# Gathering: VectorE subtracts the maxima of four of a unit's 32 experts in place, TensorE's second shift product is 384 columns wide

## The chip, the cores and the metric

The kernel runs on one core of a Trainium2 chip. The core has TensorE (matrix products; the profile calls its products PE and its weight loads PEld), VectorE (DVE), ScalarE (ACT), GpSimd (POOL) and SyncE (SP), which here only starts transfers. Each engine works through its own list of instructions in order, and semaphores are the only thing that holds one engine for another. The metric is the device time of one execution in microseconds (us), from the first to the last instruction of the core, and a little around it; less is better.

## The reference, cut to what matters

The program is one decoder block over 64 x 128 = 8192 tokens of 128 features: self attention, cross attention, and a layer of soft slots ("soft mixture of experts") with 64 experts of 32 slots each. The change lies in the last layer, in the softmax D over the slots of an expert, which weighs the tokens that are gathered into the slots:

```
logits = (jnp.einsum('tzd,ed->tze', x, phi_w) + phi_b).reshape(t, z, n, p)   # n = 64 experts, p = 32 slots
D = jax.nn.softmax(logits, axis=3)
C = jax.nn.softmax(logits, axis=2)
X_tilde = jnp.einsum('tznp,tzd->npd', D, x)
...
Y = jnp.einsum('tznp,npH->tzH', C, Y_tilde)
```

A softmax subtracts the largest logit of its group before the exponential. In D the group is the 32 slots of one expert, for each token.

## The kernel before, in words

The stages follow one another: attention, cross attention, `gather_slots` (logits, D and X_tilde), `run_experts`, `mix_slots` (C, Y and the last norm). The change touches `gather_slots` alone.

`gather_slots` goes through 128 units: 64 tiles of 128 tokens, two units to a tile, each with 32 of the 64 experts (1024 of the 2048 logits of a token). The logits of a unit lie in `psL[u % 2]`, two banks of PSUM of 512 columns: bank 0 holds the unit's experts 0 to 15, bank 1 its experts 16 to 31, 32 columns to an expert. The names in the trace are `gather_` and the name in the code (`gather_L` is `psL`, `gather_e` is `e`), and `slots_X` is `psX`, where X_tilde is summed over all tiles.

A unit u passes through these steps:

- TensorE L1009: six products of 512 columns make the logits (three terms for each bank, since x and the weights are each split into a high and a low part). The last one counts `l_made`.
- ScalarE L1035 copies half of each bank's raw logits to `keep`, bank 1 first and bank 0 after VectorE's first maximum; SyncE L993 stores them for the stage `mix_slots`. Each copy counts `kept`.
- VectorE L1067 and L1069 take the maximum of each expert's 32 slots, bank 0 and bank 1, into `mx` (count `mx_ready`).
- TensorE L1016 subtracts the maxima: two products, one a bank, of the negated identity `w.neg_ident` with `mx` spread out 32 times over (16 x 32 = 512 columns), added onto the logits in PSUM. They wait for `mx_ready` and `kept` and count `shifted`.
- ScalarE L1046 takes the exponential of both banks into `e` (count `e_ready`), VectorE L1073 sums it, waits for its own sum and inverts it (L1077, `rinv`), and GpSimd L1098 multiplies into `d`.
- The first half of `d` is split into a high part (ScalarE L1058, `dh`) and a low part (GpSimd L1092, `dl`), and so is x: ScalarE L1055 makes `x2h` and VectorE L1083 `x2l`, once a tile.
- TensorE adds to X_tilde: L1023 in full float32 with the second half of `d` (one product in the code, two instructions in the trace), L1028 to L1030 with the split parts.

The order is written by hand. In step k of the loop TensorE does the logits of unit k, the shift of unit k-1 and the sums L1023 to L1030 of unit k-4. VectorE does the maxima of unit k, then the sum and inverse of unit k-1, then `x2l` of unit k-2 where k is even. ScalarE does `keep` bank 1 of unit k, the exponential of k-1, `keep` bank 0 of k, `x2h` and `dh` of k-2. GpSimd does `dl` of unit k-3, then `d` of unit k-1. Of the waits between the steps three matter here: L1009 of unit k waits for the exponential of unit k-2 (`psL` has two halves), L1028 waits for `dl` and `x2l`, and L1073 for the exponential.

`Mix.peaks` (L1324 to L1338, in the stage `mix_slots`) is not touched. It is of interest since VectorE there subtracts maxima in place for a whole bank (L1337), right after two maxima (L1328, L1332).

Of the kernel before, what the change touches and what calls it, by code (L numbers as in the profile page):

```python
# [18 lines left out]
ALU = mybir.AluOpType  # L19
ACT = mybir.ActivationFunctionType  # L20
X = mybir.AxisListType.X
F32 = mybir.dt.float32
# [33 lines left out]
def reach(eng, sem, value):  # L56

    if not isinstance(value, int) or value > 0:
        eng.wait_ge(sem, value)  # L59
# [887 lines left out]
def gather_slots(nc, io, w, psX):  # L947
# [4 lines left out]
    TILES = TOKENS // 128  # L952
    UNITS = 2 * TILES
    KEEPS = 3
    WE_EVERY, WE_PART = UNITS // 16, EXPERTS // 16
    with ExitStack() as ctx:
        st = Store(nc, ctx, "gather")
        mx = [st.sb(f"mx{i}", [128, 2, 16], F32R) for i in range(2)]
# [8 lines left out]
        dl = [st.sb(f"dl{i}", [128, 512], F32R) for i in range(2)]  # L967
        keep = [st.sb(f"keep{i}", [128, SLOTS - MADE, 32]) for i in range(KEEPS)]
        psL = [st.ps(f"L{i}", [128, 2, 512]) for i in range(2)]
# [4 lines left out]
         x_made) = (  # L974
            st.sem(n) for n in ("l_made", "low_max", "mx_ready", "kept", "shifted", "e_ready", "sum_done", "rinv_ready",
                                "d_ready", "d_read", "dh_ready", "dl_ready", "x_made"))
        stored = [st.sem(f"stored{i}") for i in range(KEEPS)]
        block = ctx.enter_context(nc.Block())

        def units(k, lag):  # L980
            return [k - lag] if 0 <= k - lag < UNITS else []

        def rows(u):
            return slice(u // 2 * 128, u // 2 * 128 + 128)
# [3 lines left out]
        @block.sync  # L988
        def _(sync):
            by_row = io["expert_w"].rearrange("n d h -> d n h")  # L990
            for u in range(UNITS):
                sync.wait_ge(kept, 2 * u + 2)
                sync.dma_start(w.kept[rows(u), u % 2], keep[u % KEEPS][:]).then_inc(stored[u % KEEPS], 16)  # L993
                if u % WE_EVERY == WE_EVERY - 1:
                    some = slice(u // WE_EVERY * WE_PART, (u // WE_EVERY + 1) * WE_PART)
                    sync.dma_start(w.we[:, some, :], by_row[:, some, :]).then_inc(w.we_loaded, 16)
            sync.dma_start(w.beT[:], io["expert_bT"]).then_inc(w.be_loaded, 16)
            for i in range(KEEPS):
                sync.wait_ge(stored[i], 16 * len(range(i, UNITS, KEEPS)))

        @block.tensor
        def _(pe):
            for k in ORDER:
                for u in units(k, 0):
                    reach(pe, e_ready, u - 1)
                    for n, (xs, ws) in enumerate(((w.xh, w.w1h), (w.xl, w.w1h), (w.xh, w.w1l))):
                        for i in range(2):
                            c = (2 * (u % 2) + i) * 512
                            ins = pe.matmul(psL[u % 2][:, i, :], xs[:, rows(u)], ws[:, c:c + 512],  # L1009
                                            start=n == 0, stop=n == 2)  # L1010
                    ins.then_inc(l_made, 1)
                for u in units(k, 1):
                    pe.wait_ge(mx_ready, u + 1)
                    pe.wait_ge(kept, 2 * u + 2)
                    for i in range(2):
                        ins = pe.matmul(psL[u % 2][:, i, :], w.neg_ident[:],  # L1016
                                        mx[u % 2][:, i, :].unsqueeze(2).to_broadcast([128, 16, 32]), start=False,
                                        stop=True, skip_group_check=True)
                    ins.then_inc(shifted, 1)
                for u in units(k, 4):  # L1020
                    t, j, first, last = u // 2, u % 2, u < 2, u >= UNITS - 2
                    pe.wait_ge(d_ready, u + 1)
                    pe.matmul(psX[:, 2 * j + 1, :], w.xres[:, rows(u)], dd[u % 4][:, 1, :], start=first, stop=last)\  # L1023
                        .then_inc(d_read, 1)
                    pe.wait_ge(x2l_ready, t + 1)
                    pe.wait_ge(dl_ready, u + 1)
                    out = psX[:, 2 * j, :]
                    pe.matmul(out, x2h[t % 2][:], dh[j][:], start=first, stop=False)  # L1028
                    pe.matmul(out, x2h[t % 2][:], dl[j][:], start=False, stop=False)
                    pe.matmul(out, x2l[t % 2][:], dh[j][:], start=False, stop=last).then_inc(x_made, 1)  # L1030

        @block.scalar
        def _(act):
            def keep_bank(u, i):
                act.copy(keep[u % KEEPS][:, :, 16 * i:16 * i + 16],  # L1035
                         psL[u % 2][:, i, :].rearrange("t (n p) -> t p n", n=16)[:, MADE:SLOTS, :]).then_inc(kept, 1)
# [23 lines left out]
        @block.vector  # L1060
        def _(dve):
            for k in ORDER:
                for u in units(k, 0):
                    by_expert = psL[u % 2][:].rearrange("p i (n s) -> p i n s", n=16)
                    dve.wait_ge(l_made, u + 1)
                    reach(dve, shifted, u - 1)
                    dve.tensor_reduce(mx[u % 2][:, 0, :], by_expert[:, 0], X, ALU.max).then_inc(low_max, 1)  # L1067
                    dve.wait_ge(kept, 2 * u + 1)
                    dve.tensor_reduce(mx[u % 2][:, 1, :], by_expert[:, 1], X, ALU.max).then_inc(mx_ready, 1)  # L1069
                for u in units(k, 1):  # L1070
                    dve.wait_ge(e_ready, u + 1)
                    reach(dve, rinv_ready, u - 1)
                    dve.tensor_reduce(rsum[u % 2][:].rearrange("p (i n) -> p i n", i=2), e[u % 2][:], X, ALU.add)\  # L1073
                        .then_inc(sum_done, 1)
                    dve.wait_ge(sum_done, u + 1)
                    reach(dve, d_ready, u - 1)
                    dve.reciprocal(rinv[u % 2][:], rsum[u % 2][:]).then_inc(rinv_ready, 1)  # L1077
                for u in units(k, 2):
                    t = u // 2
                    if u % 2 == 0:  # L1080
                        dve.wait_ge(x2h_ready, t + 1)
                        reach(dve, x_made, u - 2)
                        dve.tensor_tensor(x2l[t % 2][:], w.xres[:, rows(u)], x2h[t % 2][:], ALU.subtract)\  # L1083
                            .then_inc(x2l_ready, 1)
# [416 lines left out]
def decoder_block(nc, io, out):  # L1501
    with ExitStack() as ctx:
# [58 lines left out]
        with ExitStack() as banks:  # L1561
            sl = Store(nc, banks, "slots")
            psX = sl.ps("X", [128, 4, 512])
            w.we = sl.sb("we", [128, EXPERTS, 128])
            w.beT = sl.sb("beT", [128, EXPERTS])
            gather_slots(nc, io, w, psX)
            w1_space.close()
            with ExitStack() as spaces:
                mix = Mix(nc, spaces, w, psX)
                run_experts(nc, w, psX, mix)  # L1570
                mix_slots(nc, w, mix, out)
# [32 lines left out]
```

## Time and profile before

| | |
|---|---|
| median of 3 runs | 1380.32 us (1377.62 to 1383.22) |
| the profiled execution | 1381.27 us |
| its span, first to last instruction | 1379.2 us |
| gathering, first to last logits product of TensorE | 458.0 to 887 us |
| TensorE products busy, whole span | 1286.2 us (93%) |
| VectorE, ScalarE, GpSimd busy | 1105.5, 896.5, 1162.0 us (80%, 65%, 84%) |
| TensorE's granted clock, mean | 0.983 of full speed |

The rows come from one profiled execution. Times are microseconds from the start of the span. In a timeline each row is one instruction, or several of the same kind merged (x2), with its start, its length and, in brackets, the idle time of its engine before it and what ended that. A product of TensorE starts while the one ahead of it still drains, so a product's length (0.39) is more than its share of the engine; the share is read from start to start. On VectorE and GpSimd too an instruction that waits for nothing starts up to 0.09 us before the end recorded for the one ahead of it.

### The profile page before, as it was taken

How to read it: one execution, taken by the hardware profiler on the slowest of the kernel's cores; microseconds unless marked ns; L12 is line 12 of the kernel's file. 1: busy time of each engine (PE TensorE's matmuls, PEld its weight loads, DVE VectorE, ACT ScalarE, POOL GpSimd, SP SyncE). 2: the span in 40 equal slices, each digit the busy share in tenths (PEclk: the TensorE clock that was granted, in tenths of full speed). 3: DMA queues.
4: the chain of work that ended last, by engine and by line, in shares of the span. 5: the costliest groups of instructions: out<-in, count | busy, mean ns of one | idle time of the engine just before them, and what ended most of it. 6: DMA issues, size and time to landing. Idle time of an engine off the chain costs nothing. (4 is left out here: it accounts for less than half of the span.)

```text
span 1379.2 us, 31693 instructions
## 1 busy us (share of the span) xinstructions
PE 1286.2 (93%) x11006; PEld 1050.8 (76%) x11006; DVE 1105.5 (80%) x2462; ACT 896.5 (65%) x1670; POOL 1162.0 (84%) x1044
## 2 busy tenths in 40 slices
PE   6785899999998799999999999969999999999998
PEld 5664677777776577777777777659999999999997
DVE  4997466666666788888888888878999999999996
ACT  3996566666666477767777677645666666666664
POOL 3666587888886599999999999958999999999997
PEclk9997899999999999999999999999999999999999
DMA  4222434434341122222222222212222222232321
GB/s 111 79 83 76 131 112 121 123 111 132 112 122 52 54 92 84 85 89 95 85 84 92 92 85 85 85 60 83 88 86 83 91 79 95 74 100 70 103 70 32
DMA packets 90963, 123.74 MB, mean 90 GB/s; under 512 B 8803, under 2 KB 62628, under 8 KB 90804
## 3 DMA queue, kind: packets, MB, share of 16 engines
q1 hardware_dynamic: 90294, 121.49, 27.9%
q8 instruction: 90, 1.47, 0.5%
q14 instruction: 67, 0.55, 0.1%
q10 hardware_dynamic: 512, 0.23, 0.1%
HBM read 70.41 MB, written 51.33 MB: 88 GB/s over the span
## 5 line engine op out<-in xcount | busy, mean ns | idle before, releaser
L1098 POOL TENSOR_TENSOR gather_d<-gather_e,gather_rinv 128x1024 f32<-128x1024 f32 x128 | 245.2, 1915 | 35.9 <-DVE gather_rinv L1077 35.9
L1357 POOL TENSOR_TENSOR mix_c<-mix_e,mix_rinv 128x1024 f32<-128x1024 f32 x128 | 241.1, 1904 | 17.9 <-DVE mix_rinv L1345 16.0
L1425 PEld LDWEIGHTS last_Y<-kept_phi,last_cT 128*128 128x128 f32 x2048 | 248.3, 192 | 7.2
L1425 PE MATMUL last_Y<-kept_phi,last_cT 128*128 128x128 f32 x2048 | 249.1, 275 | 0.0
L1441 ACT COPY last_cT<-last_T 128x1024 f32<-128x1024 f32 x128 | 128.5, 1004 | 132.4 <-PE last_T L1432 132.4
L920 POOL TENSOR_TENSOR cross_kd<-first_pack,kept_consts 128x624 fp32r<-128x624 f32 x128 | 155.7, 1238 | 59.7 <-DMA first_pack<-first_halves 54.3
L819 DVE TENSOR_REDUCE cross_mx<-cross_S 128x8 fp32r<-128x624 f32 x128 | 103.6, 809 | 107.9 <-PE cross_S L637 107.9
L1342 DVE TENSOR_REDUCE mix_sums<-mix_e 128x16 f32<-128x1024 f32 x128 | 155.8, 1217 | 34.4 <-ACT mix_e L1316 34.0
L1073 DVE TENSOR_REDUCE gather_rsum<-gather_e 128x32 f32<-128x1024 f32 x128 | 156.1, 1220 | 25.8 <-ACT gather_e L1046 25.8
L1092 POOL TENSOR_TENSOR gather_dl<-gather_d,gather_dh 128x512 fp32r<-128x512 f32 x128 | 166.3, 1299 | 0.0
L1035 ACT COPY gather_keep<-gather_L 128x256 f32<-128x256 f32 x256 | 94.8, 370 | 95.7 <-PE gather_L L1009 95.3
L1432 PE MATMUL last_T<-kept_consts,mix_c 128*128 128x128 f32 x1024 | 134.6, 275 | 3.2 <-POOL mix_c L1357 1.1
L1046 ACT ACTIVATE gather_e<-gather_L 128x1024 f32<-128x1024 f32 x128 | 131.1, 1025 | 7.4
L741 ACT ACTIVATE cross_pT<-cross_P 77x1024 f32<-77x1024 f32 x128 | 131.3, 1029 | 0.6 <-PE cross_P L657 0.6
L1023 PE MATMUL slots_X<-gather_d,kept_xres 128*128 128x512 f32 x256 | 130.7, 592 | 0.0
L1350 POOL TENSOR_TENSOR mix_less<-mix_read,mix_high 128x1024 f32<-128x1024 f32 x64 | 122.6, 1916 | 7.4 <-DVE mix_high L1332 4.1
L1432 PEld LDWEIGHTS last_T<-kept_consts,mix_c 128*128 128x128 f32 x1024 | 114.8, 142 | 4.5 <-issue 2.5
L1067 DVE TENSOR_REDUCE gather_mx<-gather_L 128x16 fp32r<-128x512 f32 x128 | 88.6, 692 | 29.6 <-PE gather_L L1009 20.7
L1028 PE MATMUL slots_X<-gather_dh,gather_x2h 128*128 128x512 f32 x128 | 101.0, 789 | 2.9 <-DVE gather_x2l L1083 1.5
L1058 ACT CAST gather_dh<-gather_d 128x512 fp32r<-128x512 f32 x128 | 79.5, 621 | 31.4 <-PE slots_X L1030 19.6
L1069 DVE TENSOR_REDUCE gather_mx<-gather_L 128x16 fp32r<-128x512 f32 x128 | 87.2, 681 | 0.0
L1009 PE MATMUL gather_L<-over_w1h,kept_xh 128*128 128x512 f32 x256 | 81.5, 400 | 4.3 <-ACT gather_e L1046 3.3
(205 smaller groups left out, 2979.6 us busy)
## 6 DMA issues: line engine op xcount, KB each, us to landing
kept_logits<-gather_keep SPq DMA_DIRECT2D x128, 256.0 KB, 2.0
mix_read<-kept_logits SPq DMA_DIRECT2D x64, 512.0 KB, 3.8
first_halves<-first_qk SPq DMA_DIRECT2D x32, 412.0 KB, 3.2
first_pack<-first_halves SPq DMA_DIRECT2D x64, 128.0 KB
first_pack<-first_halves SPq DMA_DIRECT2D x32, 206.0 KB
first_pack<-first_halves SPq DMA_DIRECT2D x64, 78.0 KB
first_xTg<-in_xT SPq DMA_DIRECT2D x16, 256.0 KB, 2.8
kept_xres<-in_x SPq DMA_DIRECT2D x16, 256.0 KB, 3.2
```

What stands on the lines that cost most here:

```text
L741: act.activation(pT[n % 2][0:J, hs, :, :], psP[:, hs, :, :], ACT.Exp)\
L920: pool.tensor_tensor(kd[n % 2][:, q], keys[:, q].to_broadcast([128, 2, 4, JP]), w.own.unsqueeze(1).unsqueeze(3).to_broadcast([128, 2, 4, J ...
L1023: pe.matmul(psX[:, 2 * j + 1, :], w.xres[:, rows(u)], dd[u % 4][:, 1, :], start=first, stop=last)\
L1046: act.activation(e[u % 2][:], psL[u % 2][:].rearrange("p i (n s) -> p i n s", n=16), ACT.Exp)\
L1073: dve.tensor_reduce(rsum[u % 2][:].rearrange("p (i n) -> p i n", i=2), e[u % 2][:], X, ALU.add)\
L1092: pool.tensor_tensor(dl[u % 2][:], dd[u % 4][:, 0, :], dh[u % 2][:], ALU.subtract).then_inc(dl_ready, 1)
L1098: pool.tensor_tensor(dd[u % 4][:].rearrange("p i (n s) -> p i n s", n=16), e[u % 2][:], rinv[u % 2][:].rearrange("p (i n) -> p i n", i=2). ...
L1342: dve.tensor_reduce(self.sums[u % 2][:], self.e[u % 2][:], X, ALU.add).then_inc(self.sum_done, 1)
L1357: pool.tensor_tensor(self.cc[u % 2][:], self.e[u % 2][:], self.rinv[u % 2][:].unsqueeze(2).to_broadcast([128, 16, EXPERTS]), ALU.mult)\
L1425: ins = pe.matmul(psY[t % 2][:, 0:128], cT[u % 2][:, c, :], w.yk[:, 8 * (u % 2) + c, :], start=(u % 2 == 0 and c == 0), stop=(u % 2 == 1 a ...
L1432: ins = pe.transpose(psT[:, c, :], mix.cc[u % 2][:, 2 * c:2 * c + 2, :], w.ident)
L1441: act.copy(cT[u % 2][:], psT[:]).then_inc(cT_ready, 1)
```

## The change

After the maxima of a unit VectorE waits for its own second maximum and then subtracts, in place in PSUM, the maxima of the unit's last four experts (experts 12 to 15 of bank 1, 4 x 32 = 128 columns). TensorE's second shift product covers the other twelve experts of that bank, 384 columns instead of 512. The first one keeps 512. TensorE waits for VectorE's new count `lowered` in place of `mx_ready`. Nothing else is different. The lines after the change are 2 higher up to the shift products and 6 higher behind VectorE's new instruction.

```diff
+    SHIFTED = 16 - 4
...
+        lowered = st.sem("lowered")
...
                 for u in units(k, 1):
-                    pe.wait_ge(mx_ready, u + 1)
+                    pe.wait_ge(lowered, u + 1)
                     pe.wait_ge(kept, 2 * u + 2)
-                    for i in range(2):
-                        ins = pe.matmul(psL[u % 2][:, i, :], w.neg_ident[:],
-                                        mx[u % 2][:, i, :].unsqueeze(2).to_broadcast([128, 16, 32]), start=False,
+                    for i, n in enumerate((16, SHIFTED)):
+                        ins = pe.matmul(psL[u % 2][:, i, 0:32 * n], w.neg_ident[:],
+                                        mx[u % 2][:, i, 0:n].unsqueeze(2).to_broadcast([128, n, 32]), start=False,
                                         stop=True, skip_group_check=True)
                     ins.then_inc(shifted, 1)
...
                     dve.tensor_reduce(mx[u % 2][:, 1, :], by_expert[:, 1], X, ALU.max).then_inc(mx_ready, 1)
+                    dve.wait_ge(mx_ready, u + 1)
+                    rest = by_expert[:, 1, SHIFTED:16]
+                    dve.tensor_tensor(rest, rest, mx[u % 2][:, 1, SHIFTED:16].bitcast(F32).unsqueeze(2)
+                                      .to_broadcast([128, 16 - SHIFTED, 32]), ALU.subtract).then_inc(lowered, 1)
```

VectorE's list in the middle of the gathering, before, from the inverse of one unit to the inverse of the second one after it:

```order
L1077 RECIPROCAL gather_rinv<-gather_rsum 128x32 [waits gather_d_ready,gather_sum_done]
L1067 TENSOR_REDUCE gather_mx<-gather_L 128x16 [waits gather_shifted,gather_l_made]
L1069 TENSOR_REDUCE gather_mx<-gather_L 128x16 [waits gather_kept]
L1073 TENSOR_REDUCE gather_rsum<-gather_e 128x32 [waits gather_rinv_ready,gather_e_ready]
L1077 RECIPROCAL gather_rinv<-gather_rsum 128x32 [waits gather_d_ready,gather_sum_done]
L1083 TENSOR_TENSOR gather_x2l<-kept_xres,gather_x2h 128x128 [waits gather_x_made,gather_x2h_ready]
```

The same place now:

```order
L1083 RECIPROCAL gather_rinv<-gather_rsum 128x32 [waits gather_d_ready,gather_sum_done]
L1069 TENSOR_REDUCE gather_mx<-gather_L 128x16 [waits gather_shifted,gather_l_made]
L1071 TENSOR_REDUCE gather_mx<-gather_L 128x16 [waits gather_kept]
L1074 TENSOR_TENSOR gather_L<-gather_L,gather_mx 128x128 [waits gather_mx_ready]
L1079 TENSOR_REDUCE gather_rsum<-gather_e 128x32 [waits gather_rinv_ready,gather_e_ready]
L1083 RECIPROCAL gather_rinv<-gather_rsum 128x32 [waits gather_d_ready,gather_sum_done]
L1089 TENSOR_TENSOR gather_x2l<-kept_xres,gather_x2h 128x128 [waits gather_x_made,gather_x2h_ready]
```

The new instruction stands between the maxima of unit k and the sum of unit k-1, and all that VectorE does later in the step stands behind it.

TensorE's list for one step of the loop, before:

```order
L1009 MATMUL gather_L<-over_w1l,kept_xh 128x512 x2
L1016 MATMUL gather_L<-gather_mx,kept_neg_ident 128x512 [waits gather_kept,gather_mx_ready]
L1016 MATMUL gather_L<-gather_mx,kept_neg_ident 128x512
L1023 MATMUL slots_X<-gather_d,kept_xres 128x512 [waits gather_d_ready]
L1028 MATMUL slots_X<-gather_dh,gather_x2h 128x512 [waits gather_dl_ready,gather_x2l_ready]
L1029 MATMUL slots_X<-gather_dl,gather_x2h 128x512
L1030 MATMUL slots_X<-gather_dh,gather_x2l 128x512
L1009 MATMUL gather_L<-over_w1h,kept_xh 128x512 [waits gather_e_ready]
```

And now:

```order
L1011 MATMUL gather_L<-over_w1l,kept_xh 128x512 x2
L1018 MATMUL gather_L<-gather_mx,kept_neg_ident 128x512 [waits gather_kept,gather_lowered]
L1018 MATMUL gather_L<-gather_mx,kept_neg_ident 128x384
L1025 MATMUL slots_X<-gather_d,kept_xres 128x512 [waits gather_d_ready]
L1030 MATMUL slots_X<-gather_dh,gather_x2h 128x512 [waits gather_dl_ready,gather_x2l_ready]
L1031 MATMUL slots_X<-gather_dl,gather_x2h 128x512
L1032 MATMUL slots_X<-gather_dh,gather_x2l 128x512
L1011 MATMUL gather_L<-over_w1h,kept_xh 128x512 [waits gather_e_ready]
```

Nothing moved on TensorE: one product has 384 columns for 512, and one wait has another name. ScalarE, GpSimd and SyncE have the same instructions in the same order as before.

## Rows read from the trace of the kernel before

**Rows 1.** Busy time by stretch: engines in order, TensorE's clock, DMA.

```profile
core 0: us, PE busy (x) PEld busy (x) DVE busy (x) ACT busy (x) POOL busy (x), PEclk, DMA share, GB/s
...
700.00:800.00 100.00, 100.00 (x388) 72.67 (x387) 86.81 (x134) 70.19 (x135) 93.87 (x61) 1.00 0.25 90
```

**Rows 2.** Who waited for whom, 471 to 889 us: total, times, longest.

```profile
POOL gather_d L1098 <- DVE gather_rinv L1077: 26.2, 123, 1.3
DVE gather_rsum L1073 <- ACT gather_e L1046: 24.7, 124, 0.2
```

**Rows 3.** Timeline of TensorE's products, one step of the loop.

```profile
703.79 0.63 PE L1009 MATMUL gather_L<-over_w1h,kept_xh 128*128 128x512 f32 x2
...
704.72 0.63 PE L1009 MATMUL gather_L<-over_w1l,kept_xh 128*128 128x512 f32 x2
705.18 0.59 PE L1016 MATMUL gather_L<-gather_mx,kept_neg_ident 128*128 128x512 f32 x2
705.62 1.02 PE L1023 MATMUL slots_X<-gather_d,kept_xres 128*128 128x512 f32 x2
...
706.93 0.40 PE L1030 MATMUL slots_X<-gather_dh,gather_x2l 128*128 128x512 f32 x1
707.17 0.62 PE L1009 MATMUL gather_L<-over_w1h,kept_xh 128*128 128x512 f32 x2
```

**Rows 4.** Timeline of cross attention: products of 312 columns, one narrower behind.

```profile
301.18 0.52 PE L637 MATMUL cross_S<-cross_kd,first_pack 128*128 128x312 f32 x2
301.54 0.38 PE L619 MATMUL cross_P<-first_xo,cross_oT 128*128 128x128 f32 x2
...
301.40 0.33 PEld L619 LDWEIGHTS cross_P<-first_xo,cross_oT 128*128 128x128 f32 x2
```

**Rows 5.** Timeline of the other engines, the same step of the loop.

```profile
702.00 0.69 DVE L1067 TENSOR_REDUCE gather_mx<-gather_L 128x16 fp32r<-128x512 f32 x1 [0.28 <-PE gather_L L1009]
...
702.43 1.02 ACT L1046 ACTIVATE gather_e<-gather_L 128x1024 f32<-128x1024 f32 x1
702.61 0.68 DVE L1069 TENSOR_REDUCE gather_mx<-gather_L 128x16 fp32r<-128x512 f32 x1
...
703.49 1.22 DVE L1073 TENSOR_REDUCE gather_rsum<-gather_e 128x32 f32<-128x1024 f32 x1 [0.20 <-ACT gather_e L1046]
703.56 0.42 PEld L1009 LDWEIGHTS gather_L<-over_w1h,kept_xh 128*128 128x128 f32 x2
...
703.68 1.31 POOL L1092 TENSOR_TENSOR gather_dl<-gather_d,gather_dh 128x512 fp32r<-128x512 f32 x1
...
704.75 0.35 DVE L1077 RECIPROCAL gather_rinv<-gather_rsum 128x32 f32<-128x32 f32 x1
...
705.01 0.23 DVE L1083 TENSOR_TENSOR gather_x2l<-kept_xres,gather_x2h 128x128 fp32r<-128x128 f32 x1
705.18 1.92 POOL L1098 TENSOR_TENSOR gather_d<-gather_e,gather_rinv 128x1024 f32<-128x1024 f32 x1 [0.20 <-DVE gather_rinv L1077]
```

**Rows 6.** VectorE's subtractions out of PSUM, by line and form, whole span.

```profile
L1337 DVE TENSOR_TENSOR slots_X<-slots_X,mix_mx 128x512 f32<-128x512 f32 x64 | 44.1, 690 | 0.0
L826 DVE TENSOR_TENSOR cross_y<-cross_P,kept_xres 128x128 f32<-128x128 f32 x61 | 17.1, 281 | 0.0
```

**Rows 7.** The start of the gathering: timeline, engines mixed.

```profile
461.58 0.68 DVE L1069 TENSOR_REDUCE gather_mx<-gather_L 128x16 fp32r<-128x512 f32 x1
...
462.57 0.59 PE L1016 MATMUL gather_L<-gather_mx,kept_neg_ident 128*128 128x512 f32 x2
...
464.28 0.73 PE L1009 MATMUL gather_L<-over_w1h,kept_xh 128*128 128x512 f32 x2 [1.11 <-ACT gather_e L1046]
...
467.49 0.73 PE L1009 MATMUL gather_L<-over_w1h,kept_xh 128*128 128x512 f32 x2 [1.11 <-ACT gather_e L1046]
```

**Rows 8.** Timeline, the last `x2l`, beside GpSimd's `dl`.

```profile
892.77 1.26 POOL L1092 TENSOR_TENSOR gather_dl<-gather_d,gather_dh 128x512 fp32r<-128x512 f32 x1
...
892.88 1.30 DVE L1083 TENSOR_TENSOR gather_x2l<-kept_xres,gather_x2h 128x128 fp32r<-128x128 f32 x1
893.99 1.96 POOL L1098 TENSOR_TENSOR gather_d<-gather_e,gather_rinv 128x1024 f32<-128x1024 f32 x1
```

## The prediction

> **What bounds the kernel now.** The change touches one stage, so I first read the table of busy time by stretch for that stage. In the 100 us from 700 to 800 TensorE is busy for all 100.00 us at its full granted clock (1.00, the 2.4 GHz level), GpSimd for 93.87, VectorE for 86.81, ScalarE for 70.19 [rows 1]. A busy TensorE may still be one that is held back in small pieces, so the second view is the timeline of its products. One step of the loop lasts from 703.79 to 707.17, 3.38 us [rows 3]. In it the six logits products take 1.39 us (703.79 to 705.18), 0.23 each, and the two shift products 0.44 us (705.18 to 705.62), 0.22 each. At 2.4 GHz 512 columns need 0.213 us, so nothing waits inside these groups; the rest of the step, 1.55 us (705.62 to 707.17), holds the full float32 product, which runs its columns four times (0.85), and three more of 0.23 (0.69), 1.54 in sum. So the step is TensorE's columns, and no wait is left in it. Third, the table of waits for 471 to 889 us: GpSimd waits 26.2 us for the inverse L1077, 0.21 us in each of 123 units, and VectorE 24.7 us for the exponential [rows 2]. Those are engines with room that wait for a step set elsewhere. A column taken from TensorE should therefore shorten the step, as long as the others keep their room.
>
> **TensorE's part.** Each unit loses 128 columns of one product. At 2.4 GHz that is 128 / 2.4 = 53 ns. The trace has no product of 384 columns in this place. The nearest rows from above are the shift products of 512 themselves, 0.22 us each [rows 3]. From below it is a product of 312 columns in cross attention: its successor's weight load begins at 301.40, as it itself begins, and the successor's product at 301.54, so 312 columns with their overhead took 0.14 us [rows 4]. From there 72 columns more are 0.03, which puts the product of 384 at 0.17 us and the gain at 0.045 to 0.05. From the 512 it is 0.16 to 0.167 and the gain 0.053. I take 0.053, since that row is the same instruction with the same operands, and keep 0.045 for the range. Over 128 units: 6.8 us, or 5.8 at the lower bound.
>
> The Trainium skill has a rule that speaks against this: "TensorE: Matmul & The Clock Gate", section "Back-to-back issue gap", gives sustained spacings of about 131 ns for 512 columns and 81 ns for 128, which is 17 ns for each 128 columns; by that the sum would be an estimated 2.1 us. The shift products' 0.22 us for 512 columns does not agree with its 131 [rows 3]; the same section's other formula, N/2.4 + 2.5 ns, does, and gives 6.8.
>
> **VectorE's part.** One instruction is added in each unit: 128 columns, one input in PSUM and one in SBUF, written to PSUM. A subtraction of this shape out of PSUM into SBUF takes 0.281 us, and the in-place one of 512 columns 0.690 [rows 6]; the slope between them is 1.07 ns a column, so the two forms lie on one line and the in-place write should cost little. I take 0.28; bounds are 0.23 (the `x2l` subtraction out of SBUF [rows 5]) and 0.35. It waits for VectorE's own last result. The sum and the inverse stand in the same relation: 703.49 + 1.22 = 704.71, and the inverse begins at 704.75 [rows 5], so 0.04 is added. Behind it the sum starts up to 0.08 before its recorded end, as L1069 does behind L1067 (702.00 + 0.69 against 702.61). Net: 0.28 + 0.04 - 0.08, about 0.24 us a unit on VectorE.
>
> Where does it fall? Counted from the start of L1067 (702.00), the second maximum ends at 1.29, the subtraction runs from 1.33 to 1.61, and the sum could start at 1.53. Before it started at 1.49, held by the exponential (702.43 + 1.02 = 703.45) [rows 5]. The exponential now ends 0.053 earlier after L1067, at 1.40. So what ends last before the sum is the new subtraction, and the sum is late by some 0.04 us against before. Then 1.22 + 0.04 + 0.35 for sum and inverse: the inverse ends at 3.14, and in a unit with `x2l` that ends at 3.14 - 0.09 + 0.23 = 3.28, with the next maximum possible from 3.20. In the other units it is possible from 3.05. The new step is 3.38 - 0.053 = 3.325. VectorE keeps 0.12 us in even units and 0.27 in odd ones; it stays hidden. If the subtraction took 0.35, even units would keep 0.05.
>
> **Who waits behind it.** TensorE: the shift of unit k-1 is issued a step later than its maxima. The maxima of the unit begin at 702.00, `lowered` would come at about 703.6, and its shift products start at 705.18 [rows 3, 5]: 1.5 us of room, so the new wait costs nothing. GpSimd: L1098 waits for the inverse (0.20 us idle before it at 705.18) and moves 0.04 later with it; from its start to the end of L1092 behind it is 1.92 + 1.31 less an overlap of about 0.04, 3.19 us against a step of 3.325 [rows 5]. It keeps some 0.13 us. TensorE's L1009 waits for the exponential, which ends at 703.45, while the weight load for L1009 comes at 703.56 [rows 5]; both move with the shift products, so those 0.1 us stay. ScalarE and SyncE get nothing new.
>
> **Ends of the stage.** The first steps are not bound by columns: L1009 starts at 464.28 and 467.49, a step of 3.21 us, after waits of 1.11 us for the exponential [rows 7]. In that loop the shift products lie too, so 0.053 is saved there as well. In the very first unit the second maximum ends at 461.58 + 0.68 = 462.26 and the shift starts at 462.57 [rows 7]; with 0.04 + 0.28 for the subtraction and a little for the signal it moves to about 462.65: 0.1 us lost once. At the end the last inverses are late by 0.04 once. Together 0.15 us. The later stages have the same work and start earlier.
>
> **The sum.** 6.8 - 0.15 = 6.6 us. Against the profiled execution: span 1379.2 - 6.6 = 1372.6, with the 2.1 us around it 1374.7. The profiled execution (1381.27) is 0.95 us above the median, so against the median I forecast 1380.32 - 6.6 = 1373.7 us. A measurement of this kernel can tell about 0.5% from no change, here 6.9 us, or 1373.4: my forecast is 0.48% and lies right at that line.
>
> **Rivals.**
>
> 1. *The weight load becomes the floor.* A weight load of 128 columns is recorded with 0.19 us (0.42 for two that start 0.23 apart [rows 5]), longer than the 0.16 of the new product. If the product behind could not start before its load's recorded end, the slot would be 0.19 and the gain 0.03 a unit, 3.8 us: 1376.5. Against it: at 301.40 such a load begins and the product that uses it starts 0.14 us later [rows 4].
>
> 2. *Another engine takes over the step.* GpSimd and VectorE have only some 0.13 us left. Should the subtraction and its waits cost VectorE 0.4 us a unit and not 0.24, the even units alone would grow and eat the gain of the odd ones: about 1380, no change. For it: VectorE's room is the smallest of all. Against it: each term has a row of its own kind.
>
> 3. *Slower: `x2l` meets GpSimd.* `x2l` (L1083) reads two operands from SBUF. At 892.88 it was issued while GpSimd's L1092 ran (892.77 to 894.03) and took 1.30 us, not 0.23: it sat until that one was nearly over [rows 8]. In the steady state it falls into the gap that GpSimd leaves while it waits for the inverse: L1092 ends at 704.99, `x2l` runs from 705.01, L1098 starts at 705.18 [rows 5]. This gap shrinks by 0.05. If L1098 came to read first, `x2l` would wait for all of it, and 1.9 - 0.12 = 1.8 us would be added to every second unit: 64 x 1.8 = 115 us, 1489. It decides at `x2l` being issued after L1098, which means 0.17 us later against it than now. Both follow the same inverse, so their distance stays, and at 892.88 the waiting `x2l` ended at 894.18, well inside L1098 (893.99 to 895.95), so it was served first [rows 8]. I expect it to be met by the end of L1092 at worst, for hundredths.
>
> The Trainium skill states the mechanism ("SBUF — State Buffer", section "Who interferes with whom"): a VectorE instruction with two SBUF inputs contends with GpSimd instructions that read SBUF, and who starts first holds the other off. The row at 892.88 agrees. By the same section the new subtraction, with one input in PSUM, is not concerned.
>
> **How the numbers follow.** Forecast mechanism (TensorE's columns, 5.7 to 7.0 us): 0.80. Rival 1: 0.08. Rival 2: 0.07. Rival 3: 0.05. The three runs before lie from 2.7 below to 2.9 above their median, and a median of new runs may be off by some 1.5. The forecast's 6.6 against the line at 6.9 puts the 0.80 at about one half each: 0.40 faster by over 0.5%, 0.40 within. Rivals 1 and 2 are within 0.5% (0.15), though 0.01 of rival 2 is slower. So faster 0.40, same 0.54, slower 0.06. Range: from 1373.7 - 0.4 - 2.7 = 1370.6 to rival 1 with some scatter, 1376.5 + 2.1 = 1378.6; rivals 2 and 3 are left out.
>
> **What would show it.** The step of TensorE in the middle of the stage is 3.32 to 3.33 us, and the second shift product's slot 0.16; the weight load's floor would show as 0.19 with a step of 3.35. The new VectorE instruction reads 0.27 to 0.30 us. The idle time before the sum moves from the exponential to nothing, and `x2l` stays near 0.23. GpSimd's wait for the inverse falls from 0.21 to about 0.15. If `x2l` reads well over 0.3 us, rival 3 is at work; if TensorE waits for `lowered`, my room of 1.5 us was wrong. The logits products would end some 6.6 us earlier, and every later stage be unchanged in length.

## The result: 1372.96 us, and the profile after

| | before | after |
|---|---|---|
| median of 6 runs | 1380.1 us (1377.62 to 1383.22) | 1372.96 us (1368.54 to 1375.12) |
| ratio, 95% interval | | 0.995 (0.9938 to 0.9963) |
| span of the profiled execution | 1379.2 us | 1371.7 us |
| first and last start of the first maximum (L1067, now L1069) | 461.0 and 887.7 us | 460.2 and 880.4 us |

The forecast was 1373.7 us, 6.6 less than before; the medians differ by 7.1. The last row of the table holds the gathering, from its first unit to its last: 426.7 us before and 420.2 now, 6.5 less. Between these two profiled executions another 0.8 us lies before the stage began, where both kernels have the same code, and 0.2 behind it.

Where the 6.5 us went is seen in the timeline of TensorE's products in the changed kernel, one step of the loop (L1011 makes the logits, L1018 is the shift, L1025 the float32 product, L1030 to L1032 the split ones):

```profile
704.07 0.54 PE L1018 MATMUL gather_L<-gather_mx,kept_neg_ident 128*128 128x512 f32 x2
704.44 1.02 PE L1025 MATMUL slots_X<-gather_d,kept_xres 128*128 128x512 f32 x2
704.90 0.80 PE L1030 MATMUL slots_X<-gather_dh,gather_x2h 128*128 128x512 f32 x1
705.54 0.40 PE L1031 MATMUL slots_X<-gather_dl,gather_x2h 128*128 128x512 f32 x1
705.77 0.40 PE L1032 MATMUL slots_X<-gather_dh,gather_x2l 128*128 128x512 f32 x1
706.01 0.62 PE L1011 MATMUL gather_L<-over_w1h,kept_xh 128*128 128x512 f32 x2
706.46 0.63 PE L1011 MATMUL gather_L<-over_w1h,kept_xl 128*128 128x512 f32 x2
706.93 0.62 PE L1011 MATMUL gather_L<-over_w1l,kept_xh 128*128 128x512 f32 x2
707.39 0.54 PE L1018 MATMUL gather_L<-gather_mx,kept_neg_ident 128*128 128x512 f32 x2
```

The step is 707.39 - 704.07 = 3.32 us, where [rows 3] had 3.38. The two shift products take 704.07 to 704.44, 0.37 us and not 0.44; the merged row names only the first one's 512 columns. Everything else has its old spacing. TensorE is busy for the whole stretch as before:

```profile
core 0: us, PE busy (x) PEld busy (x) DVE busy (x) ACT busy (x) POOL busy (x), PEclk, DMA share, GB/s
700.00:800.00 100.00, 100.00 (x393) 72.94 (x393) 94.25 (x166) 71.65 (x136) 95.38 (x61) 1.00 0.24 88
```

Against [rows 1] VectorE rose from 86.81 to 94.25 us of 100, and GpSimd from 93.87 to 95.38, since its same work now fits into shorter steps. VectorE and GpSimd in the same step:

```profile
703.72 0.35 DVE L1083 RECIPROCAL gather_rinv<-gather_rsum 128x32 f32<-128x32 f32 x1
...
704.15 1.91 POOL L1104 TENSOR_TENSOR gather_d<-gather_e,gather_rinv 128x1024 f32<-128x1024 f32 x1 [0.16 <-DVE gather_rinv L1083]
...
704.26 0.69 DVE L1069 TENSOR_REDUCE gather_mx<-gather_L 128x16 fp32r<-128x512 f32 x1 [0.19 <-PE gather_L L1011]
...
704.87 0.68 DVE L1071 TENSOR_REDUCE gather_mx<-gather_L 128x16 fp32r<-128x512 f32 x1
...
705.59 0.30 DVE L1074 TENSOR_TENSOR gather_L<-gather_L,gather_mx 128x128 f32<-128x128 f32 x1
...
705.80 1.21 DVE L1079 TENSOR_REDUCE gather_rsum<-gather_e 128x32 f32<-128x1024 f32 x1
...
707.04 0.35 DVE L1083 RECIPROCAL gather_rinv<-gather_rsum 128x32 f32<-128x32 f32 x1
...
707.31 0.23 DVE L1089 TENSOR_TENSOR gather_x2l<-kept_xres,gather_x2h 128x128 fp32r<-128x128 f32 x1
```

The new subtraction takes 0.30 us, starts 0.04 behind the end of the maximum ahead of it (704.87 + 0.68 = 705.55), and the sum follows without a wait. In [rows 5] the sum started 1.49 us after the first maximum; now it is 705.80 - 704.26 = 1.54. The table of waits, 471 to 882 us, says who still waits; against [rows 2] the sum's wait for the exponential is gone, and GpSimd's wait for the inverse is listed for 86 units where it was for 123:

```profile
POOL gather_d L1104 <- DVE gather_rinv L1083: 13.4, 86, 0.2
DVE gather_mx L1069 <- PE gather_L L1011: 11.7, 61, 0.2
```

The view leaves out waits under 0.15 us. Over the units 8 to 119 GpSimd sat idle before `d` for 0.204 us in the mean before the change and for 0.154 after it.

### The profile page after: what moved, and what is told of

It reads as the page before. It is cut to its first block and busy times, and to the rows that moved or that the text cites. A ratio compares the mean times of both kernels' runs of the same rounds, so it can differ in the third digit from the quotient of the medians.

```text
span 1371.7 us, 31821 instructions
## 1 busy us (share of the span) xinstructions
PE 1279.5 (93%) x11006; PEld 1048.0 (76%) x11006; DVE 1129.5 (82%) x2590; ACT 896.0 (65%) x1670; POOL 1160.2 (85%) x1044
## 5 line engine op out<-in xcount | busy, mean ns | idle before, releaser
L1025 PE MATMUL slots_X<-gather_d,kept_xres 128*128 128x512 f32 x256 | 130.8, 593 | 0.0
L1069 DVE TENSOR_REDUCE gather_mx<-gather_L 128x16 fp32r<-128x512 f32 x128 | 88.5, 692 | 18.6 <-PE gather_L L1011 15.3
L1030 PE MATMUL slots_X<-gather_dh,gather_x2h 128*128 128x512 f32 x128 | 101.0, 789 | 2.9 <-POOL gather_dl L1098 2.9
L1011 PE MATMUL gather_L<-over_w1h,kept_xh 128*128 128x512 f32 x256 | 80.9, 398 | 4.3 <-ACT gather_e L1048 3.3
```

## The experiments

The main theory is that of the prediction: the step of the gathering is TensorE's columns, and VectorE's subtraction is hidden. The rivals were a cost of the subtraction on the path, the weight load as a floor, another engine taking over, and `x2l` meeting GpSimd. In the tables "step" is the mean distance from one start of the first maximum to the next over the units 5 to 123 of the profiled execution, 3.377 us before and 3.323 after the change. Ratios are against the kernel before on the same chip, whose median there was 1378.96 us for the first four runs (four experts with 512 columns, 384 columns alone, eight experts, the whole bank), 1380.4 for 256 and 64 columns alone, and 1379.77 for the others.

### Each half of the change alone

First, the subtraction on VectorE with the product of 512 columns kept:

```diff
-                    for i, n in enumerate((16, SHIFTED)):
+                    for i, n in enumerate((16, 16)):
```

> VectorE subtracts the four experts' maxima as in the changed kernel, and TensorE's second shift product keeps its 512 columns (so the four experts are shifted twice, which a softmax does not notice). Theory (the step of the gathering is TensorE's columns, VectorE's new instruction is hidden): the step stays at 3.38 us and the time at that of the kernel before, 1380 us, ratio 0.998 to 1.002. Rival (VectorE's instruction costs something on the path): over 1382 us, and TensorE or GpSimd waits longer.

Measured: 1379.71 us, ratio 1.0005 (0.9992 to 1.0017), step 3.377 us. Second, the narrow product with nobody subtracting the rest:

```diff
-                    pe.wait_ge(lowered, u + 1)
+                    pe.wait_ge(mx_ready, u + 1)
...
-                    dve.wait_ge(mx_ready, u + 1)
-                    rest = by_expert[:, 1, SHIFTED:16]
-                    dve.tensor_tensor(rest, rest, mx[u % 2][:, 1, SHIFTED:16].bitcast(F32).unsqueeze(2)
-                                      .to_broadcast([128, 16 - SHIFTED, 32]), ALU.subtract).then_inc(lowered, 1)
```

> TensorE's second shift product has 384 columns and nobody subtracts the maxima of the other four experts: that part of the shift is left out. Theory (columns alone): the step is 3.32 us and the time that of the changed kernel, 1373 us, within 1 us. Rival (VectorE's subtraction costs part of the gain): this one is faster than the changed kernel by 2 us or more.

Measured: 1371.23 us, ratio 0.9944 (0.9929 to 0.9958), step 3.323 us, the same to the nanosecond as that of the changed kernel. The two ratios, 0.9944 here and 0.995 for the change, lie within each other's intervals. The median is 1.7 us lower than that of the changed kernel and the "within 1 us" of the expectation was missed. The kernel before is 1.1 us lower in this comparison too (1378.96 against 1380.1), the runs scatter by some 3 us, and the stage is not shorter (L1069's first and last start):

```profile
L1069 DVE TENSOR_REDUCE gather_mx<-gather_L x128: 690/692/692, 459.3 to 880.0; 128x16 fp32r<-128x512 f32 x128
```

That is 420.7 us, against 420.2 with the subtraction. The whole gain is in the columns, and the subtraction costs nothing that these runs can show. The waits of the first experiment (subtraction and 512 columns) show the same from the other side: GpSimd's wait for the inverse is back at 0.21 us a unit (25.0 us in 119), as in [rows 2].

```profile
POOL gather_d L1104 <- DVE gather_rinv L1083: 25.0, 119, 0.2
```

### More experts on VectorE: how far the room goes

The runs with eight and with six experts are the changed kernel with another number in one line, for eight:

```diff
-    SHIFTED = 16 - 4
+    SHIFTED = 16 - 8
```

> As the changed kernel, with eight experts on VectorE and 256 columns in the second product. Theory: TensorE's step is 3.323 - 0.053 = 3.27 us; VectorE needs 0.13 us more a unit, 3.33 in even and 3.18 in odd units, 3.26 in the mean, so it has just no room left and does not yet set the step; 1366.5 us, ratio 0.990. Rival (VectorE's even units count one by one, or GpSimd is pushed): a step of 3.30 us or more, 1370 us or above.

> As the changed kernel, with six experts on VectorE and 320 columns in the second product. Theory: TensorE's columns set the step at 3.323 - 0.027 = 3.297 us, VectorE needs 3.27 and 3.11 us in even and odd units; 1370 us, ratio 0.993. Rival (the even units with x2l already hold the step): 3.32 us and 1373 us.

| experts on VectorE, columns of the second product | time | ratio (95%) | step |
|---|---|---|---|
| 4, 384 (the change) | 1372.96 | 0.995 (0.9938 to 0.9963) | 3.323 |
| 6, 320 | 1369.48 | 0.9924 (0.9912 to 0.9937) | 3.295 |
| 8, 256 | 1368.83 | 0.9922 (0.9909 to 0.9934) | 3.278 |
| 16, none | 1394.36 | 1.0107 (1.0094 to 1.0121) | 3.476 |

With six the step is what the columns give (3.297 was expected). With eight it is 3.278 where 3.27 was expected. Its time missed the expected 1366.5 us by 2.3: the stage, from the first maximum to the last, takes 414.98 us against 420.24 in the changed kernel, 5.3 less and not 6.8, and the rest is within the scatter of the medians. By their times six and eight cannot be told apart. With eight the step is no longer even: the distances from maximum to maximum alternate between 3.164 and 3.392 us (means over odd and even units). VectorE is now the one without room, and it meets GpSimd. Timeline of VectorE and GpSimd in the run with eight:

```profile
701.54 1.92 POOL L1104 TENSOR_TENSOR gather_d<-gather_e,gather_rinv 128x1024 f32<-128x1024 f32 x1 [0.23 <-DVE gather_rinv L1083]
...
703.41 1.28 POOL L1098 TENSOR_TENSOR gather_dl<-gather_d,gather_dh 128x512 fp32r<-128x512 f32 x1
...
704.48 0.35 DVE L1089 TENSOR_TENSOR gather_x2l<-kept_xres,gather_x2h 128x128 fp32r<-128x128 f32 x1
704.65 1.97 POOL L1104 TENSOR_TENSOR gather_d<-gather_e,gather_rinv 128x1024 f32<-128x1024 f32 x1
704.76 0.68 DVE L1069 TENSOR_REDUCE gather_mx<-gather_L 128x16 fp32r<-128x512 f32 x1
```

`x2l` is issued at 704.48, while GpSimd's `dl` (703.41 to 704.69) still runs; it takes 0.35 us and not 0.23, and GpSimd's next product is recorded with 1.97 and not 1.92. VectorE loses 0.12 us and GpSimd 0.05 in every second unit, and the mean step is only 0.005 us over that of 256 columns with nothing on VectorE (3.273, below).

All sixteen experts of the bank on VectorE, without the second product:

```diff
-    SHIFTED = 16 - 4
+    SHIFTED = 16 - 16
...
-                    for i, n in enumerate((16, SHIFTED)):
+                    for i, n in enumerate((16,)):
```

> As the changed kernel, with all sixteen experts of bank 1 on VectorE and no second product. Theory: TensorE's columns would allow 3.38 - 0.22 = 3.16 us, but VectorE's subtraction grows from 0.30 to 0.69 us and VectorE needs 3.59 and 3.43 us in even and odd units; the step is 3.51 us and the time 1380 + 128 x 0.13 = 1397 us, ratio 1.012. Rival (columns alone count): 3.19 us, held by GpSimd, 1356 us.

Measured: 1394.36 us, ratio 1.0107, step 3.476 us. Here VectorE sets the step alone: its subtraction is 0.70 us, and TensorE waits for it in each unit. From the table of waits of that run, 471 to 880 us:

```profile
POOL gather_d L1104 <- DVE gather_rinv L1083: 39.5, 118, 1.5
ACT gather_keep L1037 <- DVE gather_mx L1069: 35.8, 118, 0.3
PEld gather_L L1018 <- DVE gather_L L1074: 26.9, 118, 0.3
```

The expected 3.51 was 0.035 too long. The first maximum is recorded with 0.653 us in the mean here against 0.692, which is about as much; both it and the second (0.68) follow at once on other work here. Steps of 3.431 and 3.520 alternate.

The last of this group asks whether a single unit in which VectorE is too slow holds the step, or only the mean. VectorE subtracts eight experts and TensorE keeps 384 columns:

```diff
-    SHIFTED = 16 - 4
+    SHIFTED = 16 - 8
...
-                    for i, n in enumerate((16, SHIFTED)):
+                    for i, n in enumerate((16, 12)):
```

> VectorE subtracts eight experts as in the run with eight, TensorE's second product keeps 384 columns (four of the eight are shifted twice, which a softmax does not notice). VectorE needs 3.33 us in even and 3.18 us in odd units against 3.323 of TensorE. If only the mean over two units counts, the step stays at 3.323 and the time at 1373 us. If an even unit that is too long holds TensorE, the step alternates and its mean is over 3.33 us, 1374 us or more.

Measured: 1374.82 us, ratio 0.9966 (0.9954 to 0.9979), step 3.321 us. VectorE needs an estimated 3.33 us in every second unit and the mean step is still TensorE's 3.32. A margin of 0.01 us is thin by itself. The run with eight experts and 256 columns says it more clearly: its long units take 3.392 us, 0.12 over TensorE's 3.273, and the mean of long and short is 3.278. So the mean over two units counts. In the run with 384 columns VectorE is busy for 97.05 of the 100 us from 700 to 800, 2.8 more than after the change, and the step is the same. The time is 1.8 us over the expectation of 1373, within the scatter of the runs; the stage takes 420.4 us against 420.2 in the changed kernel, so the profile shows no cause for it there.

### What `x2l` costs when it meets GpSimd

In the changed kernel `x2l` keeps its length (min/median/max in ns, 64 of them):

```profile
L1089 DVE TENSOR_TENSOR gather_x2l<-kept_xres,gather_x2h x64: 226/228/334, 468.4 to 885.5; 128x128 fp32r<-128x128 f32 x64
```

So the rival did not occur, and its price was made visible by moving `x2l` between the two maxima of the next step (the last tile's `x2l` is done apart):

```diff
                     dve.tensor_reduce(mx[u % 2][:, 0, :], by_expert[:, 0], X, ALU.max).then_inc(low_max, 1)
+                    if k % 2 == 1 and k >= 3:
+                        t = (k - 3) // 2
+                        dve.wait_ge(x2h_ready, t + 1)
+                        reach(dve, x_made, 2 * t - 2)
+                        dve.tensor_tensor(x2l[t % 2][:], w.xres[:, rows(2 * t)], x2h[t % 2][:], ALU.subtract)\
+                            .then_inc(x2l_ready, 1)
...
-                        dve.tensor_tensor(x2l[t % 2][:], w.xres[:, rows(u)], x2h[t % 2][:], ALU.subtract)\
-                            .then_inc(x2l_ready, 1)
```

> As the changed kernel, with VectorE's x2l issued in the next step, between its two maxima, when GpSimd is in the middle of its product d. This pays the price of the rival in which x2l meets GpSimd. If x2l waits for the whole of d: x2l is recorded with 1.1 to 1.6 us, VectorE needs 7.4 to 7.6 us for two units, the step is 3.7 to 3.85 us in the mean and the time 1420 to 1440 us. If two inputs in SBUF do not collide with GpSimd here, x2l stays at 0.23 us and the time at 1373 us.

Measured: 1440.04 us, ratio 1.0429 (1.0412 to 1.0445), step 3.850 us, 4.725 and 2.975 in turn. Timeline of GpSimd and VectorE:

```profile
699.62 1.92 POOL L1108 TENSOR_TENSOR gather_d<-gather_e,gather_rinv 128x1024 f32<-128x1024 f32 x1
699.86 1.82 DVE L1074 TENSOR_TENSOR gather_x2l<-kept_xres,gather_x2h 128x128 fp32r<-128x128 f32 x1
...
701.50 1.32 POOL L1102 TENSOR_TENSOR gather_dl<-gather_d,gather_dh 128x512 fp32r<-128x512 f32 x1
...
701.61 0.68 DVE L1077 TENSOR_REDUCE gather_mx<-gather_L 128x16 fp32r<-128x512 f32 x1
```

`x2l` was issued 0.24 us behind the start of GpSimd's `d` and ended at 701.68, 0.14 behind its end: 1.82 us for an instruction of 0.23, more than the 1.1 to 1.6 that were expected; the step and the time lie at the upper end of what was expected. The maxima (0.63 to 0.68) and the sums (1.21), with one input, run beside GpSimd no longer than usual. The same instruction issued 0.16 us ahead of `d`, as in the changed kernel, costs nothing that shows, and 0.24 behind it the whole kernel takes 67 us more than the changed one. It was said ahead of the prediction that semaphores are the only thing that holds one engine for another; [rows 8] and this run show an engine that is held without one.

### The floor under a short product

With the rest of the shift left out and VectorE out of the question, how short can the second product become?

```diff
-    SHIFTED = 16 - 4
+    SHIFTED = 16 - 12
```

(16 - 8 and 16 - 14 for the other two, each also without VectorE's subtraction, as in the second experiment.)

> TensorE's second product has 128 columns and nobody subtracts the maxima of the other twelve experts, which leaves that part of the shift out. It looks for the next bound behind the columns. TensorE's columns alone would give 3.38 - 0.16 = 3.217 us and 1359.6 us. GpSimd needs 1.915 + 1.30 - 0.04 - 0.04 = 3.14 us if x2l never keeps it waiting and some 3.19 if it does. Expected: 3.22 us a step, 1360 us; if the loop over GpSimd and x2l sets in earlier, 3.25 us or more and over 1363 us.

> TensorE's second product has 256 columns and nobody subtracts the maxima of the other eight experts, which leaves that part of the shift out. If a weight load takes 0.108 us of its own way, as in the run with 128 columns, and 256 columns take 0.107, load and product are just as long and the step is 3.27 us, 1366.5 us: the same as with 128 columns. Against the run with eight experts on VectorE it also shows what VectorE costs there (step 3.278): nothing that can be measured. If the floor were GpSimd's, this run would have the same step, but the one with 64 columns tells that apart.

> The same with 64 columns. With the weight load as the floor the step stays at 3.27 us and the float32 product behind the short one starts early and is recorded with 0.65 to 0.68 us (it sits until its load is done). With columns alone it would be 3.19 us and 1356 us.

| columns of the second product, nothing on VectorE | time | ratio (95%) | step |
|---|---|---|---|
| 384 | 1371.23 | 0.9944 (0.9929 to 0.9958) | 3.323 |
| 256 | 1368.42 | 0.9917 (0.9898 to 0.9935) | 3.273 |
| 128 | 1367.07 | 0.9907 (0.9894 to 0.9921) | 3.273 |
| 64 | 1366.97 | 0.991 (0.9888 to 0.9932) | 3.273 |

The expectation for 128 columns was wrong: 3.217 us and 1360 us were expected, and 3.273 and 1367.07 measured. From 256 columns down the step does not move any more. Of the run with 128 columns, TensorE's products:

```profile
706.20 0.43 PE L1018 MATMUL gather_L<-gather_mx,kept_neg_ident 128*128 128x512 f32 x2
706.47 1.08 PE L1025 MATMUL slots_X<-gather_d,kept_xres 128*128 128x512 f32 x2
...
707.61 0.40 PE L1031 MATMUL slots_X<-gather_dl,gather_x2h 128*128 128x512 f32 x1
```

and its weight loads:

```profile
706.41 0.30 PEld L1025 LDWEIGHTS slots_X<-gather_d,kept_xres 128*128 128x128 f32 x2
706.95 0.19 PEld L1030 LDWEIGHTS slots_X<-gather_dh,gather_x2h 128*128 128x128 f32 x1 [0.24 <-issue]
```

The pair of float32 products begins early, at 706.47, but the first of them is stretched (the pair is 1.08 us long, where it is 1.02 after 384 columns), and L1031 comes 1.14 us after L1025's start, not 1.10. The two loads for the pair are 0.30 long together and a single one is 0.19 (second row), so one starts 0.11 us behind the other: loads follow at 0.11 us at the least, and a product shorter than that leaves TensorE with nothing to run. With 384 columns the same two loads are 0.16 apart:

```profile
704.28 0.35 PEld L1025 LDWEIGHTS slots_X<-gather_d,kept_xres 128*128 128x128 f32 x2
```

With 64 columns the float32 products have a mean of 633 ns against 593 with 256, and the step is the same to the nanosecond.

The starts of the products say it without the recorded lengths. From the start of the short product to that of the first float32 one it is 162, 109, 56 and 29 ns with 384, 256, 128 and 64 columns, and from there to the second one 429, 431, 484 and 511: 591 in sum with 384, and 540 with each of the others. A floor set by another engine would show as TensorE waiting for that engine, and the tables of waits of these runs have no such row in the middle of the stage. GpSimd, the busiest of the other engines, sits idle for 0.10 us before each `d` in all three. Against 256 columns with eight experts on VectorE (3.278) the run with 256 alone also shows what VectorE costs there: 0.005 us a step.

The floor is 3.323 - 3.273 = 0.050 us below the changed kernel, 0.16 - 0.05 = 0.11 us for the short product. The kernel before had it on show, in the stretch of [rows 4]. Its L619 row holds two products of 128 columns, and the next product, of 128 columns too and with a load of its own, is this:

```profile
301.76 0.27 PE L627 MATMUL cross_P<-kept_consts,kept_xres 128*128 128x128 f32 x1
```

The three start at 301.54, 301.65 and 301.76, 0.11 us apart, where their columns alone would give 0.053 by the prediction's own working.

The Trainium skill gives the time of a load ("TensorE: Matmul & The Clock Gate", section "LDWEIGHTS (loading the stationary operand)": P columns divided by 1.2, an estimated 107 ns for 128 columns). The trace agrees, with 0.11 from load to load. That a shorter product is held by it is what these runs show. The recorded length of 0.19 is not the floor.

## Why the prediction was right

**What bounds the kernel.** That TensorE's columns are the step held in every run from 512 columns down to 256 in which VectorE had room: 0.053 us for each 128 columns gives 3.323, 3.297 and 3.270 for 384, 320 and 256, and 3.323, 3.295 and 3.273 were measured. It was read from spacings that leave no gap, not from "busy 100 us": in the run with 64 columns TensorE is as busy and a part of it is stretched time.

**TensorE's part.** 0.053 us a unit was forecast and 3.377 - 3.323 = 0.054 measured. The slot of the second shift product, from start to start, is 0.162 us, where 0.16 was forecast. This also rules out the 2.1 us that the prediction names as what a smaller gain per column would give. The lower bound of 0.045, from the product of 312 columns, was too low; why that product has some 0.01 us more of overhead was not looked into.

**VectorE's part.** The subtraction was put at 0.28 us and took 0.30 (299 ns in the mean), 18 ns more than the row of the same size that writes to SBUF. The prediction had inferred from two rows that both forms "lie on one line", but two points always do. The runs have the in-place form in four widths, 299, 366, 432 and 699 ns for 128, 192, 256 and 512 columns, and the in-place row of [rows 6], 690 for 512, spreads each maximum over 64 columns and not 32. Whether the write to PSUM or the second operand, spread out there and plain in the other, makes the 18 ns was not tested. The sum was to start 1.53 us after the first maximum and starts at 1.54. The room was 0.12 us in even units; both halves alone show that none of this reached the step.

**The waits.** TensorE never waited for `lowered` in the middle of the stage. GpSimd's idle time before `d` fell from 0.204 to 0.154 us, with 0.15 forecast. `x2l` stayed at 0.228.

**The sum.** 6.6 us forecast, 6.5 in the stage between the first and last maximum, 7.5 between the spans of the two profiled executions, 7.1 between the medians. Of the 1.0 us that the spans have over the stage 0.8 lies ahead of it, where the first maximum begins at 460.2 against 461.0 us; in the ten other profiles of unchanged early stages it begins anywhere from 457.4 to 461.2, so this is scatter. The ends of the stage were put at 0.15 us of loss. The first five units take 14.80 us before and 14.79 after, where some 0.17 less was forecast; the same five take 14.0 to 15.3 in the runs with nothing on VectorE, so this term is too small to be judged. With the ratio at 0.995 the gain lies on the bound of 0.5%, as forecast, and its interval covers both sides of it.

**The rivals.** The weight load is a floor, but at 0.11 us, not at the 0.19 of its record, so it did not bind at 384 columns and does below 256; my rival was right that a load can be the floor and took the wrong length for it. Another engine taking over begins at about eight experts, where VectorE waits for no other engine any more and the step is 3.278 us against 3.273 without it, and is plain at sixteen. The price of that rival was wrong: it named 0.4 us of VectorE's time a unit as the point at which the whole gain is eaten. The run with eight experts and 384 columns has it, 0.433 + 0.04 - 0.08 = 0.39 us, and kept the step of 3.321 us, since the odd units lend their room to the even ones. `x2l` meeting GpSimd was priced at 1.8 us for each second unit and 115 us; when forced it cost 67 us. Its 1.8 us of added wait came out as 1.6 (1.82 us against 0.23), and two steps together grew by only 2 x (3.850 - 3.323) = 1.05 us. VectorE's room in the two, 0.12 + 0.27 by the prediction, takes up 0.39 of the difference; the other 0.15 is not accounted for. `x2l` also stood at another place in VectorE's list than in the rival.

## What to carry to other kernels

When TensorE is bound by its columns and each product has a weight load of its own, a narrower product pays by the column only down to the time from one load to the next, 0.11 us here for 128 columns. It is read from the starts of short products that follow one another, as the kernel before already had them, and not from a load's recorded length. The work that is moved over is free as long as the receiving engine's mean over the loop's period stays below the step; here six or eight experts instead of four gave 10 us and not 7, and sixteen lost 15. Where the receiving engine's work alternates from unit to unit, its longest unit is the wrong thing to compare with the step. A VectorE instruction with two SBUF operands is best issued ahead of a long GpSimd instruction that reads SBUF and not behind its start; the runs show this for one pair of instructions.

## What the runs showed of the hardware that was not expected

- The load-to-load floor of 0.11 us on TensorE, which shows as a longer product behind the short one (mean of both float32 products 633 against 593 ns; the first of them alone 674 against 594) and not as a wait.
- VectorE's `x2l` beside GpSimd's `d`: 1.82 us for 0.23 when issued 0.24 us behind the start of `d`, and nothing when issued 0.16 ahead of it; what lies between was not measured. Where it comes while the preceding `dl` ends, it costs 0.12 us (0.35 against 0.23) and GpSimd 0.05.
- A unit in which VectorE is slower than TensorE costs next to nothing when the next one has room: 3.392 and 3.164 us in turn give a step of 3.278 against TensorE's 3.273, and 3.321 us a step stand with VectorE busy 97% of the time.
